# A CIN and MLP kernel: a pair in three groups instead of four, other row pairs copied, and rows taken directly for the first two pairs

## The chip, the core and the metric

The kernel runs on one core of one Trainium2 chip, with its engines TensorE (PE in the profile; PEld is its weight load), VectorE (DVE), ScalarE (ACT), GpSimd (POOL) and SyncE (SP), and the core's 16 DMA engines. The metric is the device time of one execution in microseconds, as the median of a few runs.

## The reference

An xDeepFM network on 512 samples: 26 embedding rows of 32 numbers each, two layers of a compressed interaction network (CIN), a deep network of three layers, and a linear part. Constants: B = 512, M = 26, E = 32, ND = 13, layers of 128 outputs in the CIN, 1024, 512 and 256 in the deep network.

```python
emb = tables[feat_idx, sparse]                     # (B, 26, 32)
linear_out = lin_sparse_w[feat_idx, sparse].sum(-1) + dense @ lin_dense_w
x0 = xk = emb
for w, bb in ((conv1_w, conv1_b), (conv2_w, conv2_b)):
    h = xk.shape[1]
    hp = jnp.einsum('bhd,bmd->bhmd', xk, x0).reshape(-1, h * M, E)
    xn = jax.nn.sigmoid(jnp.einsum('oi,bid->bod', w, hp) + bb[None, :, None])
    half = xn.shape[1] // 2
    xk = xn[:, :half]
    res.append(xn[:, half:])
cin_out = (jnp.concatenate(res, axis=1).sum(-1) @ cin_w + cin_b)[:, 0]
deep_x = jnp.concatenate([emb.reshape(-1, M * E), dense], axis=-1)
h1 = jnp.tanh(deep_x @ W1 + b1)
h2 = jnp.tanh(h1 @ W2 + b2)
h3 = jnp.tanh(h2 @ W3 + b3)
return linear_out + cin_out + (h3 @ deep_w + deep_b)[:, 0] + bias[0]
```

## The kernel before

**Tiling.** The 512 samples are cut into 16 pairs of blocks (`NPAIR`); a block has 16 samples, which are 512 columns (`CH`, 16 samples by 32 dimensions). The two blocks of a pair are called c = 0 and 1. GpSimd gathers the rows of pair i with seven indirect DMAs (`gather`, line 372) into `emb`, where a partition is one field of one sample. SyncE writes them to `laid` in HBM, one row per field (`lay_out`, lines 293 and 295), and reads them back in two forms: as `raw`, 26 rows in four places (`fetch`, line 307), and as `copied`, each of two rows spread over 64 partitions (`copy`, line 318; 512 KB for one tile in two transfers). `x` is made from `raw`: ScalarE's `x_high` (line 611) rounds it to the fast format, VectorE's `x_low` (line 730) puts the rest beside it, so that `x` holds a high and a low part of each row.

**First CIN layer.** By squares: `sums_of(i, u)` (line 439, three for each pair) forms sums of two rows with a selection matrix, `squares` (line 620) squares them, `layer1(i, c)` (line 457, twelve matmul records each) multiplies them by weights, `sigmoid(i, c)` (lines 631 and 633) gives `xk` and `res1`.

**Second CIN layer.** Thirteen tiles for each pair, of two rows of x0 by 64 rows of `xk`. The left factor of a tile is either one of `copied`, from the DMA, or is spread by TensorE with `spread_tile` (line 469) from `x` into a PSUM bank; `COPIED` and `SPREAD` say which. VectorE multiplies it by `xk` (line 800), and `main(r)` (line 479, four matmul records) adds weights times product to the bank `conv`. Then `sigmoid2` (line 641) and the folds over dimensions (`fold1_of`, `fold2_of`, lines 738 and 744).

**Deep network.** The weights of layer 1 are split into high and low parts piece by piece (`piece_high`, `piece_low`), one piece for each pair from pair 1 on. `turn` (lines 757 and 758) transposes `emb` into `xt`; ScalarE makes `xt_hi` (line 695) and GpSimd `xt_lo` (line 381); for the last pair they are made apart (lines 698, 699 and 388). `deep(layer, mt)` (line 500) multiplies in three passes: high by high, low by high, high by low; `deep(0, 0)` has 21 matmuls.

**Order.** Each engine's order is written out by hand. From pair 1 on TensorE goes through `GROUPS` (lines 563 to 575): for each group first the sums of a later pair (`SUMS_IN`) and the spreads (`SPREADS_IN`), then the tiles of the group, then one half of the next pair's layer 1 after groups 0 and 1 (`L1_IN`). Pair 0 has an order of its own (lines 543 to 561). Sums and spreads share three PSUM slots of two banks in turn (`RING`): a slot taken by a spread is free when VectorE has multiplied it, one taken by sums when ScalarE has squared them. Sums and spreads use 58 rows at partition 0 and 58 at partition 64, so c = 0 and c = 1 run in two row halves; `main` and `layer1` use 64 weight columns each, in two column halves. There are six `copied` buffers (`RC`) for seven copied tiles in a pair: `copy(n)` waits for `main` of the tile of copy n - 6, and SyncE issues everything in order, with `lay_out(i + 3)` after the second and `fetch(i + 3)` before the fifth copy of a pair. There are three `prod` buffers (`RP`), one of which is free when `main` of the spread tile three earlier is done. VectorE goes through tiles 0 to 12, with side work behind certain tiles (lines 803 to 814). GpSimd's `gather(i)` waits until the rows of pair i - 1 are in. `WARM` matmuls run at the start on data that is at hand.

## Time and profile before

| | |
|---|---|
| runs | 426.15, 426.61, 427.26 us, median 426.61 |
| profiled execution | 427.28 us, its span 425.20 us |
| PE busy | 406.2 us (96%) |
| DVE busy | 312.3 us (73%) |
| ACT busy | 160.9 us (38%) |
| POOL busy | 166.6 us (39%) |
| moved by DMA | 74.12 MB, mean 174 GB/s |
| products of the second layer, line 479 | 832 matmul records |
| layer 1, line 457 | 384 matmul records |
| spreads (line 469), sums (line 439) | 192 and 96 matmul records |

Times in the trace are microseconds from the start of the span. Consecutive matmuls overlap, so a row's length is more than its share of TensorE's time; from one start to the next is what it takes. A row with `x12` stands for twelve instructions in a run.

### The profile page before, as it was taken

Reading aid. Unit: us, or ns where it says so; the run is one execution under the profiler, and the core shown is the slowest. Engines: PE = TensorE matmul, PEld = TensorE weight load, DVE = VectorE, ACT = ScalarE, POOL = GpSimd, SP = SyncE. Lnnn points to the kernel's source line nnn. Section 1 sums busy time; section 2 is a strip of 40 time slices with the busy share of each in tenths; the row PEclk is TensorE's granted clock in tenths of the full one; section 3 lists DMA queues with packets and bytes.
Section 4 is the critical chain, followed back from the end, with each engine's and each line's share of the span. In section 5 each row is a group of like instructions: output and inputs, shape, how many; then the busy total and the mean of one; then the engine's idle time right before and its main releaser. Section 6 shows DMA issues by size and latency. Waiting matters only on the chain.

```text
span 425.2 us, 5237 instructions
## 1 busy us (share of the span) xinstructions
PE 406.2 (96%) x1850; PEld 164.2 (39%) x1850; DVE 312.3 (73%) x345; ACT 160.9 (38%) x269; POOL 166.6 (39%) x148
## 2 busy tenths in 40 slices
PE   3968999989999999999999999999999989999997
PEld 1322333323333333333333333333333326887885
DVE  4006977979989889898989898988989893732223
ACT  3054343435444435436262534443543601111112
POOL 6752662463643735645748340000000371870000
PEclk9996999999999999999999999999999999999999
DMA  5458679998999999999899999988876940330000
GB/s 200 84 119 184 162 168 226 228 228 216 227 239 236 237 226 231 232 223 237 212 233 221 229 211 229 216 207 205 208 193 163 224 115 0 102 98 2 0 0 1
DMA packets 42176, 74.12 MB, mean 174 GB/s; under 512 B 20593, under 2 KB 23025, under 8 KB 42150
## 3 DMA queue, kind: packets, MB, share of 16 engines
q1 hardware_dynamic: 38566, 72.03, 71.1%
q0 software_dynamic: 3584, 1.76, 3.1%
q8 instruction: 14, 0.23, 0.2%
q14 instruction: 12, 0.10, 0.1%
HBM read 72.06 MB, written 1.71 MB: 173 GB/s over the span
## 4 chain that ended last, share of the span: by engine, by line
PE 77%; DMA 8%; POOL 6%; DVE 4%; issue 3%; SPq 2%; DVEq 0%
PE conv L479 36%; PE conv L457 16%; PE conv L500 8%; PE ring L500 7%; POOL emb L372 6%; PE ring L469 5%; DMA emb<-in_table,rows 4%; PE ring L439 4%; DMA copied<-laid 4%; DVE copied L800 2%; SPq L318 1%; DVE prod L800 1%; PE ring L514 1%; DMA idx_sb<-in_idx 0%; SPq L307 0%
## 5 line engine op out<-in xcount | busy, mean ns | idle before, releaser
L372 POOL DMA_INDIRECT emb<-in_table,rows x112 | 133.9, 1196 | 114.8 <-DMA emb<-in_table,rows 83.1
L800 DVE TENSOR_TENSOR copied<-copied,xk 128x1024 f32<-128x1024 f32 x112 | 134.0, 1226 | 5.4 <-DMA copied<-laid 5.2
L800 DVE TENSOR_TENSOR prod<-ring,xk 128x1024 f32<-128x1024 f32 x96 | 115.4, 1220 | 30.2 <-PE ring L469 28.3
L479 PE MATMUL conv<-copied,w_sb 128*64 128x512 f32 x448 | 105.9, 594 | 3.9 <-DVE copied L800 3.7
L479 PE MATMUL conv<-prod,w_sb 128*64 128x512 f32 x384 | 98.5, 619 | 1.1 <-DVE prod L800 1.1
L631 ACT ACTIVATE xk<-conv,const_sb 64x512 f32<-64x512 f32 x64 | 43.6, 682 | 128.9 <-PE conv L457 128.0
L457 PE MATMUL conv<-sq,w_sb 117*64 117x512 f32 x384 | 88.1, 593 | 0.3 <-ACT sq L660 0.3
L620 ACT ACTIVATE sq<-ring 117x512 f32<-117x512 f32 x90 | 48.6, 594 | 27.3 <-PE ring L439 25.2
L479 PEld LDWEIGHTS conv<-copied,w_sb 128*64 128x64 f32 x448 | 31.2, 137 | 69.5 <-issue 46.2
L457 PEld LDWEIGHTS conv<-sq,w_sb 117*64 117x64 f32 x384 | 27.2, 136 | 54.2 <-issue 54.0
L381 POOL TENSOR_TENSOR xt_lo<-xt,xt_hi 128x480 fp32r<-128x480 f32 (+1 forms) x7 | 9.4, 1366 | 88.7 <-ACT xt_hi L695 84.1
L479 PEld LDWEIGHTS conv<-prod,w_sb 128*64 128x64 f32 x384 | 22.0, 137 | 42.3 <-issue 34.3
L469 PE MATMUL ring<-x,sel_sb 58*128 58x512 f32 x192 | 35.7, 419 | 0.7 <-ACT sq L620 0.7
L730 DVE SCALAR_TENSOR_TENSOR x<-raw,const_sb,x 122x512 fp32r<-122x512 f32 x16 | 12.0, 751 | 23.7 <-ACT x L611 23.7
L439 PE MATMUL ring<-x,sel_sb 58*117 58x512 f32 x96 | 23.6, 494 | 3.7 <-DVE x L730 3.7
L469 PEld LDWEIGHTS ring<-x,sel_sb 58*128 58x128 f32 x192 | 16.8, 186 | 21.2 <-issue 16.2
L439 PEld LDWEIGHTS ring<-x,sel_sb 58*117 58x117 f32 x96 | 8.7, 178 | 42.0 <-issue 38.7
L633 ACT ACTIVATE res<-conv,const_sb 64x512 f32<-64x512 f32 x32 | 21.8, 683 | 0.8
L835 DVE CAST h_hi<-hf 128x512 fp32r<-128x512 f32 x8 | 8.6, 1075 | 18.0 <-ACT hf L711 18.0
L641 ACT ACTIVATE res<-conv,const_sb 128x512 f32<-128x512 f32 x16 | 11.0, 688 | 22.9 <-PE conv L479 22.9
L611 ACT ACTIVATE x<-raw 122x512 fp32r<-122x512 f32 x16 | 10.2, 636 | 21.6 <-DMA raw<-laid 21.5
L744 DVE TENSOR_REDUCE fold<-res 128x16 f32<-128x512 f32 x16 | 10.2, 639 | 6.6 <-ACT res L641 6.6
(98 smaller groups left out, 298.7 us busy)
## 6 DMA issues: line engine op xcount, KB each, us to landing
copied<-laid SPq DMA_DIRECT2D x224, 256.0 KB, 5.5
wpiece<-in_mlp SPq DMA_DIRECT2D x22, 256.0 KB
raw<-laid SPq DMA_DIRECT2D x64, 52.0 KB
emb<-in_table,rows POOLq DMA_INDIRECT x112
laid<-emb SPq DMA_DIRECT2D x16, 96.0 KB
sel_f<-in_sel SPq DMA_DIRECT2D x1, 832.0 KB, 6.1
const_sb<-in_const SPq DMA_DIRECT2D x1, 626.5 KB, 4.5
w_sb<-in_w SPq DMA_DIRECT2D x1, 416.0 KB, 6.6
```

The source lines that it names most:

```text
L372: pool.indirect_dma_start(out=emb[0:n, i, j, :], out_offset=None, in_=table, in_offset=bass.IndirectOffsetOnAxis(ap=rows[0:n, i, j:j + 1], ...
L439: mm = nc.tensor.matmul(sums_bank(i, u)[0:UK, c, :], sel1_sb[at:at + XK, u, :], x[i % RX][at:at + XK, :], start=True, stop=True)
L457: mm = nc.tensor.matmul(l1_bank(i, c)[o, :], w1_sb[:, u, o], sq[i % 2][0:UK, u, c, :], start=(u == 0), stop=(u == UT - 1))
L469: mm = nc.tensor.matmul(spread_bank(r)[:, c, :], sel2_sb[at:at + XK, t, :], x[i % RX][at:at + XK, :], start=True, stop=True)
L479: mm = nc.tensor.matmul(conv[i % 2][c * HALF:(c + 1) * HALF, :], w2_sb[:, t, :], prod_of(r)[:, c, :], start=(t == 0), stop=(t == T2 - 1))
L500: mm = nc.tensor.matmul(MLP_BANKS[n % 2], w[0:r, k, mt * P:(mt + 1) * P], h[0:r, k, :], start=(k == 0 and j == 0), stop=(k == kt - 1 and j ...
L620: nc.scalar.activation(sq[i % 2][0:UK, u, c, :], sums_bank(i, u)[0:UK, c, :], ACT.Square)\
L631: nc.scalar.activation(xk[i % 2][q * HALF:(q + 1) * HALF, c, :], bank[0:HALF, :], ACT.Sigmoid, bias=small_sb[0:HALF, C_CB1:C_CB1 + 1]).the ...
L633: nc.scalar.activation(res1[i % 2][c * HALF:(c + 1) * HALF, :], bank[HALF:P, :], ACT.Sigmoid, bias=small_sb[HALF:P, C_CB1:C_CB1 + 1]).then ...
L641: nc.scalar.activation(res2[i % 2][:, :], conv[i % 2][:, :], ACT.Sigmoid, bias=small_sb[:, C_CB2:C_CB2 + 1]).then_inc(l2_read, 1)
L730: nc.vector.scalar_tensor_tensor(x[i % RX][0:XEND, :], raw[i % RX][0:XEND, :], small_sb[0:XEND, C_LOW:C_LOW + 1], x[i % RX][0:XEND, :].bit ...
L800: nc.vector.tensor_tensor(prod_of(r)[:, :, :].rearrange("p c n -> p (c n)"), left[:, :, :].rearrange("p c n -> p (c n)"), xk[i % 2][:, :, ...
```

## The change

The tiles are grouped 4, 5 and 4 instead of 4, 4, 4 and 1, and each group is preceded by one sum and two spreads. Which tiles are copied changes with it: 2, 3, 6, 7, 8, 11, 12 (seven as before). ScalarE's squares and sigmoids of the next pairs stand in the new order. In the last pair `deep(0, 0)` is cut into three parts by `DEEP_IN`, one behind each group, each waiting for the `xt_lo` it reads; the last pair is turned in pair 14, `xt_hi` and `xt_lo` are made whole (seven each), and the folds of pair 14 (second) and 15 come behind the products. For pairs 0 and 1 the rows go from `emb` straight into a staging tile `wide` (the buffers copied4 and copied5, until `x_lo` of the pair is made) by seven transfers that each wait for their own gather, instead of through `laid` and `raw`; `x_high` and `x_low` are then two instructions each, one for each block. Pair 0's and 1's `lay_out` stays, for the copies. Two matmuls on weights, whose result is not used, stand before the first sums of pair 1.

```diff
@@ -36,18 +36,19 @@
...
+DIRECT = 2
...
-COPIED = (2, 3, 5, 6, 7, 10, 11)
+COPIED = (2, 3, 6, 7, 8, 11, 12)
...
-DEEP_AT = 2
-GROUPS = ((0, 1, 2, 3), (4, 5, 6, 7), (8, 9, 10, 11), (12,))
-SPREADS_IN = (((0, 4),), ((0, 8), (0, 9)), ((0, 12), (1, 0)), ((1, 1),))
-SUMS_IN = {0: ((1, 2),), 2: ((2, 0),), 3: ((2, 1),)}
+DEEP_IN = {0: (0, 1), 1: (2, 3), 2: (4, 5, 6)}
+GROUPS = ((0, 1, 2, 3), (4, 5, 6, 7, 8), (9, 10, 11, 12))
+SPREADS_IN = (((0, 4), (0, 5)), ((0, 9), (0, 10)), ((1, 0), (1, 1)))
+SUMS_IN = {0: ((1, 2),), 1: ((2, 0),), 2: ((2, 1),)}
...
@@ -206,6 +208,20 @@
...
+        def wait_rows(eng, i):
+
+            if i < DIRECT:
+                for j in range(GJ):
+                    eng.wait_ge(early_in[i][j], 16)
+            else:
+                eng.wait_ge(rows_in[i % GSEM], ROWS * (i // GSEM + (1 if i % GSEM >= DIRECT else 0)))
+
+        wide = [copied[RC - DIRECT + k] for k in range(DIRECT)]
+
+        def raw_landed(i):
+
+            return RAW * (i // RX + (1 if i % RX >= DIRECT else 0))
...
@@ -289,11 +305,19 @@
 
             def lay_out(i):
 
-                sp.wait_ge(rows_in[i % GSEM], ROWS * (i // GSEM + 1))
+                wait_rows(sp, i)
...
+            def direct(i):
+
+                for j in range(GJ):
+                    m = GM if j < NG else ML
+                    sp.wait_ge(early_in[i][j], 16)
+                    sp.dma_start(wide[i][j * GM:j * GM + m, :, :].rearrange("p c n -> p (c n)"),
+                                 emb[0:m * PB, i, j, 0:E]).then_inc(wide_in[i], 16)
...
@@ -314,6 +338,8 @@
                 if n >= RC:
                     sp.wait_ge(main_done, tile_of_copy(n - RC) + 1)
                 sp.wait_ge(laid_in[i % RX], LAID * (i // RX + 1))
+                if RC - DIRECT <= n < RC:
+                    sp.wait_ge(x_lo_done, n - (RC - DIRECT) + 1)
...
@@ -324,12 +350,12 @@
...
+            direct(0)
             lay_out(0)
-            fetch(0)
             for n in range(2):
                 copy(n)
+            direct(1)
             lay_out(1)
-            fetch(1)
...
@@ -363,30 +389,21 @@
...
-                if i >= GSEM:
-                    pool.wait_ge(rows_in[i % GSEM], ROWS * (i // GSEM))
                 if i >= 2:
-                    pool.wait_ge(rows_in[(i - 1) % GSEM], ROWS * ((i - 1) // GSEM + 1))
+                    wait_rows(pool, i - 1)
...
+                    ).then_inc(early_in[i][j] if i < DIRECT else rows_in[i % GSEM], 16)
...
@@ -401,16 +418,15 @@
...
-            pool.wait_ge(prod_done, T2 * (NPAIR - 2) + 12)
-            for k in range(3):
+            pool.wait_ge(prod_done, T2 * (NPAIR - 1))
+            for k in range(2):
                 xt_low(k)
             pool.wait_ge(prod_done, T2 * (NPAIR - 1) + 4)
-            for k in range(3, 5):
+            for k in range(2, 4):
                 xt_low(k)
-            pool.wait_ge(prod_done, T2 * (NPAIR - 1) + 8)
-            for k in range(5, K1):
+            pool.wait_ge(prod_done, T2 * (NPAIR - 1) + 9)
+            for k in range(4, K1):
                 xt_low(k)
-            xt_low_rest()
...
@@ -483,16 +499,16 @@
...
-            def deep(layer, mt):
+            def deep(layer, mt, ks=None):
 
                 hi, lo, kt, xh, xl = deep_layers[layer]
                 start = sum(MT[:layer])
                 n = start + mt
-                if n == 0:
-                    pe.wait_ge(xt_lo_done, K1 + 2)
                 if n >= 2:
                     pe.wait_ge(tanh_done, n - 1)
-                for k in range(kt):
+                for k in range(kt) if ks is None else ks:
+                    if n == 0:
+                        pe.wait_ge(xt_lo_done, k + 1)
...
@@ -500,7 +516,8 @@
...
-                mm.then_inc(mlp_done, 1)
+                if ks is None or ks[-1] == kt - 1:
+                    mm.then_inc(mlp_done, 1)
...
@@ -540,6 +557,10 @@
...
+            slot_free("sums", 1, 0)
+            for k in range(2):
+                nc.tensor.matmul(sums_bank(1, 0)[:, 0, :], w2_sb[:, 0:2, :].rearrange("p t o -> p (t o)"),
+                                 w2_sb[:, 0:8, :].rearrange("p t o -> p (t o)"), start=True, stop=True)
             for u in range(UT):
                 sums_of(1, u)
                 main(u)
...
@@ -567,10 +588,11 @@
...
-                    if i == NPAIR - 1 and g == DEEP_AT:
-                        pe.wait_ge(piece_lo, KW)
-                        pe.wait_ge(l2_read, NPAIR - 1)
-                        deep(0, 0)
+                    if i == NPAIR - 1 and g in DEEP_IN:
+                        if g == 0:
+                            pe.wait_ge(piece_lo, KW)
+                            pe.wait_ge(l2_read, NPAIR - 1)
+                        deep(0, 0, DEEP_IN[g])
...
@@ -603,7 +625,14 @@
...
-                act.wait_ge(raw_in[i % RX], RAW * (i // RX + 1))
+                if i < DIRECT:
+                    act.wait_ge(wide_in[i], 16 * GJ)
+                    act.wait_ge(zeroed, 2 + i)
+                    for c in range(2):
+                        nc.scalar.activation(x[i][HALF * c:HALF * c + M, :], wide[i][0:M, c, :], ACT.Copy, scale=-1.0)\
+                          .then_inc(x_hi_done, 1)
+                    return
+                act.wait_ge(raw_in[i % RX], raw_landed(i))
...
@@ -682,21 +711,20 @@
...
                 if i + 1 < NPAIR:
                     sigmoid(i + 1, 0)
+                if i + 2 < NPAIR:
+                    squares(i + 2, 0)
+                if i + 1 < NPAIR:
                     sigmoid(i + 1, 1)
                 if i + 2 < NPAIR:
-                    squares(i + 2, 0)
                     squares(i + 2, 1)
...
-                    act.wait_ge(turned, 2 * (NPAIR - 1))
+                    act.wait_ge(turned, 2 * NPAIR)
...
                     for k in range(K1):
                         n = P if k < K1 - 1 else K1_LAST
-                        nc.scalar.activation(xt_hi[0:n, k, 0:XT], xt[0:n, k, 0:XT], ACT.Copy).then_inc(xt_hi_done, 1)
-
-            act.wait_ge(turned, 2 * NPAIR)
-            nc.scalar.activation(xt_hi[:, 0:NG, XT:B], xt[:, 0:NG, XT:B], ACT.Copy).then_inc(xt_hi_done, 1)
-            nc.scalar.activation(xt_hi[0:K1_LAST, NG, XT:B], xt[0:K1_LAST, NG, XT:B], ACT.Copy).then_inc(xt_hi_done, 1)
+                        nc.scalar.activation(xt_hi[0:n, k, :], xt[0:n, k, :], ACT.Copy).then_inc(xt_hi_done, 1)
...
@@ -726,7 +754,15 @@
...
-                dve.wait_ge(x_hi_done, i + 1)
+                if i < DIRECT:
+                    for c in range(2):
+                        at = HALF * c
+                        dve.wait_ge(x_hi_done, 2 * i + c + 1)
+                        low = nc.vector.tensor_tensor(x[i][at + XLO:at + XK, :], wide[i][0:M, c, :],
+                                                      x[i][at:at + M, :].bitcast(F32), ALU.add)
+                    low.then_inc(x_lo_done, 1)
+                    return
+                dve.wait_ge(x_hi_done, DIRECT + i + 1)
...
@@ -804,16 +840,20 @@
...
-                    if t == FOLD1_AT[k]:
+                    if t == FOLD1_AT[k] and i < NPAIR - 1:
                         fold1_of(i)
-                    if t == (0 if i == NPAIR - 1 else TURN_AT):
+                    if t == TURN_AT and i < NPAIR - 1:
                         turn(i)
-                    if t == TURN_AT and i:
+                        if i == NPAIR - 2:
+                            turn(NPAIR - 1)
+                    if t == TURN_AT and 0 < i < NPAIR - 1:
                         fold2_of(i - 1)
...
             nc.vector.tensor_reduce(lin[:, :], emb[:, :, 0:NG, E], AX.X, ALU.add).then_inc(lin_step, 1)
+            fold2_of(NPAIR - 2)
+            fold1_of(NPAIR - 1)
             fold2_of(NPAIR - 1)
             dve.wait_ge(fold1_done, NPAIR)
```

## Rows read from the trace of the kernel before

**Rows 1.** The page: granted clock in 40 slices, and the queue of the gathers.

```profile
PEclk9996999999999999999999999999999999999999
...
q0 software_dynamic: 3584, 1.76, 3.1%
```

**Rows 2.** Busy time of each engine in two stretches, clock, DMA share, GB/s.

```profile
119.64:139.41 19.77, 19.77 (x97) 6.44 (x98) 17.76 (x19) 9.04 (x16) 8.97 (x8) 1.00 1.02 234
...
258.05:277.83 19.78, 19.78 (x97) 6.44 (x98) 17.76 (x19) 8.97 (x16) 0.00 (x0) 1.00 0.92 218
```

**Rows 3.** The chain that ended last, one pair: start us, us, what.

```profile
218.51 1.01 PE conv L479 x4
220.18 3.58 PE conv L479 x16
223.76 2.58 PE conv L457 x12
226.33 0.67 PE ring L469 x3
...
233.16 0.42 PE ring L439 x2
...
234.04 3.58 PE conv L479 x16
238.28 1.01 PE conv L479 x4
```

**Rows 4.** Timeline of one pair: start, us, what [idle before].

```profile
198.78 1.23 DVE L800 TENSOR_TENSOR prod<-ring,xk 128x1024 f32<-128x1024 f32 x1 [1.90 <-PE ring L469]
...
199.92 2.35 DVE L800 TENSOR_TENSOR copied<-copied,xk 128x1024 f32<-128x1024 f32 x2
...
213.44 1.39 ACT L631 ACTIVATE xk<-conv,const_sb 64x512 f32<-64x512 f32 x2 [4.73 <-PE conv L457]
```

**Rows 5.** Line 318 (`copied`) from 100 to 120 us: issue to landing.

```profile
DMA to landing us min/median/max: 3.5/6.4/9.2
```

**Rows 6.** Timeline of the start, from `laid` of pair 1 to tile 0.

```profile
25.59 0.40 SPq L293 DMA_DIRECT2D laid<-emb  x1
...
27.82 1.54 SPq L307 DMA_DIRECT2D raw<-laid  x4
...
31.13 0.63 ACT L611 ACTIVATE x<-raw 122x512 fp32r<-122x512 f32 x1 [3.35 <-DMA raw<-laid]
...
33.21 2.36 DVE L800 TENSOR_TENSOR prod<-ring,xk 128x1024 f32<-128x1024 f32 x2 [0.66 <-ACT xk L631]
...
34.58 1.97 PE L479 MATMUL conv<-prod,w_sb 128*64 128x512 f32 x4 [1.10 <-DVE prod L800]
```

**Rows 7.** Timeline in pairs 1 and 2, and the chain before pair 3.

```profile
54.06 0.39 SPq L293 DMA_DIRECT2D laid<-emb  x1
...
58.80 0.49 PE L439 MATMUL ring<-x,sel_sb 58*117 58x512 f32 x2
...
68.45 1.23 DVE L800 TENSOR_TENSOR copied<-copied,xk 128x1024 f32<-128x1024 f32 x1 [1.14 <-DMA copied<-laid]
...
89.81 1.23 DVE L800 TENSOR_TENSOR copied<-copied,xk 128x1024 f32<-128x1024 f32 x1 [1.32 <-DMA copied<-laid]
...
99.87 1.01 PE conv L479 x4
```

**Rows 8.** Timeline and chain in pair 15, and the page's `xt_lo`.

```profile
337.63 0.51 PE L469 MATMUL ring<-x,sel_sb 58*128 58x512 f32 x2
...
337.88 2.88 DVE L800 TENSOR_TENSOR copied<-copied,xk 128x1024 f32<-128x1024 f32 x2
...
352.89 5.02 PE conv L500 x21
...
359.19 0.50 PE L500 MATMUL ring<-xt_hi,m_hi 128*128 128x512 f32 x1
...
L381 POOL TENSOR_TENSOR xt_lo<-xt,xt_hi 128x480 fp32r<-128x480 f32 (+1 forms) x7 | 9.4, 1366 | 88.7 <-ACT xt_hi L695 84.1
```

More of the change, by code:

```diff
@@ L161, in build @@
         rows_in = [sem(f"rows_in{k}") for k in range(GSEM)]
+        wide_in = [sem(f"wide_in{k}") for k in range(DIRECT)]
+        early_in = [[sem(f"early_in{i}_{j}") for j in range(GJ)] for i in range(DIRECT)]
         laid_in = [sem(f"laid_in{k}") for k in range(RX)]
@@ L189, in build @@
         HT = sum(MT)
-        XT = PB * (NPAIR - 1)
         BH = B // 2
@@ L374, in gather @@
                         in_offset=bass.IndirectOffsetOnAxis(ap=rows[0:n, i, j:j + 1], axis=0),
-                    ).then_inc(rows_in[i % GSEM], 16)
+                    ).then_inc(early_in[i][j] if i < DIRECT else rows_in[i % GSEM], 16)
             def xt_low(k):
@@ L380, in xt_low @@
                 pool.wait_ge(xt_hi_done, k + 1)
-                nc.gpsimd.tensor_tensor(xt_lo[0:n, k, 0:XT], xt[0:n, k, 0:XT], xt_hi[0:n, k, 0:XT].bitcast(F32),
+                nc.gpsimd.tensor_tensor(xt_lo[0:n, k, :], xt[0:n, k, :], xt_hi[0:n, k, :].bitcast(F32),
                                         ALU.subtract).then_inc(xt_lo_done, 1)
-            def xt_low_rest():
-                for j, (n, ks) in enumerate(((P, slice(0, NG)), (K1_LAST, slice(NG, K1)))):
-                    pool.wait_ge(xt_hi_done, K1 + j + 1)
-                    nc.gpsimd.tensor_tensor(xt_lo[0:n, ks, XT:B], xt[0:n, ks, XT:B], xt_hi[0:n, ks, XT:B].bitcast(F32),
-                                            ALU.subtract).then_inc(xt_lo_done, 1)
             def split_piece(k):
@@ L753, in turn @@
             def turn(i):
-                dve.wait_ge(rows_in[i % GSEM], ROWS * (i // GSEM + 1))
+                wait_rows(dve, i)
                 at = i * PB
```

## The prediction

> **What bounds the kernel now.** I read the busy time by stretches first, one stretch per pair of batch blocks. From pair 3 on a pair takes 19.77 us, and TensorE is busy in all of it at full clock, VectorE in 17.76, ScalarE in 9 [rows 2]. The DMA engines stand at a share of about 1.0 while rows are gathered, and at 0.92 once the gathers are over [rows 2]; yet the period is the same in both. So TensorE sets the period, and the DMA engines are close behind it.
>
> Next the chain of waits over one pair shows what TensorE's time is made of [rows 3]. Products (L479) and layer 1 (L457) use two column halves; row-sums (L439) and spreads (L469) use two row halves. Twelve matmuls of layer 1 take 2.58 us, 0.215 each. Sixteen of products should then take 3.44 and take 3.58; four should take 0.86 and take 1.01: entering a column stretch costs 0.145. The row stretches last 0.66 (from 219.52 to 220.18: one sum, one spread), 0.67 (two spreads), 0.88 (a sum, two spreads) and 0.66 (237.62 to 238.28). That fits 0.215 for each sum or spread and 0.235 for entering. One change to rows and back costs 0.38 us, and a pair has four.
>
> Last I read the start and the end. The start waits for data: VectorE's first product begins at 33.21, behind rows that go gather, `laid` in HBM, `raw`, `x` [rows 6], and even in pairs 1 and 2 it waits for copies [rows 7]. In pair 15 no layer 1 is left and VectorE is the limit: its products with their side work end at 352.89, and only then come `deep(0, 0)` and the last product [rows 8].
>
> **Steady pairs.** The work per pair is the same: 13 products and 6 blocks of layer 1 (76 matmuls), 3 sums, 6 spreads. With three stretches: 76 x 0.215 + 3 x 0.145 + 9 x 0.215 + 3 x 0.235 = 19.41 us, against 19.77. Taken from the four stretches themselves, the saving is 0.38; I use 0.37. It holds only if nothing else comes late, so I lay out the new pair, with T = 0 at its first row stretch:
> - Rows 0 to 0.88, products 0-3 and layer 1 to 7.04, rows to 7.92, products 4-8 and layer 1 to 14.94, rows to 15.82, products 9-12 to 19.4.
> - ScalarE needs 1.39 after the second layer 1 for the next pair's `xk` [rows 4], so VectorE's product 0 of the next pair begins at 14.94 + 0.1 + 1.4 = 16.45, which is -2.95 in that pair. Products start 1.13 apart (two in 2.35) [rows 4]. Products 1 to 3 begin at -1.8, -0.7, 0.4; 4 and 5 at 1.6 and 2.7; then `x_low` and `fold1`; 6 to 8 at 5.2, 6.3, 7.5; 9 at 8.6; turn and `fold2`; 10 to 12 to 14.8. The idle 19.41 - 17.76 = 1.65 lies before the next product 0, where 1.90 lies now [rows 4].
> - TensorE wants product 3 at 3.6 (there at 1.6), 8 at 11.5 (there at 8.7), product 4's and 5's banks at 7.04 (free at 3.9), `x_low` of pair i+2 at 7.04 instead of in the third group (there at 4.6). All have 2.4 us or more. Squares follow ScalarE's new order, which is that of the stretches. I charge nothing.
> - Copies: a buffer is free when the tile six copies earlier is multiplied. Tile 8's copy is released at 18.6 (tile 11 done) and its second half issued at 19.8; VectorE wants it at 19.4 + 7.5 = 26.9, 7.1 later, and TensorE suffers only when it lands after 29.6, 9.8 later. Tile 3's has 8 and 10.7. Landings take 6.4 in the middle and 9.2 at worst where transfers are dense [rows 5]. So lateness reaches VectorE and is taken up there.
>
> The saving counts for pairs 3 to 14: 12 x 0.37 = 4.4 us. DMA demand: 0.92 x 19.78 = 18.2 us of engine time per pair without gathers, plus the gathers' 3.1% of 425 over 16 pairs, 0.8 [rows 1, 2]: 19.0 of 19.4. It fits narrowly. For pairs 3 to 8, which still carry the backlog of the start, I take 0.5 off.
>
> **The start.** `direct` takes `x` of pairs 0 and 1 straight from `emb`. Pair 0 gains little, since the warm-up matmuls, the aux product and the sums follow each other on TensorE to 21.5: at most 0.5. Pair 1: the last rows are in at 25.6; now 1.8 us pass from issuing `laid` to issuing `raw`, and `raw` is in by 31.1 [rows 6]. The direct transfers of six blocks have been issued as they came, and only the last small one remains. No row shows such a transfer; the `laid` store reads the same 128-byte pieces and needs 1.8, which I take, between 1 and 4. Then 25.6 + 0.4 + 1.8 = 27.8. Two activations of 512 columns at 0.63 (now one) to 29.1, the sigmoids 1.4: the first product begins at 30.6, 2.6 earlier. The two matmuls put before `sums_of(1, 0)` lie in the idle time before 30 and keep TensorE busy: the first two products of pair 0 now take 1.97 us for four matmuls instead of about 1.0, at a granted clock of 0.6 in that slice [rows 1, 6]. That returns up to 1.8, and pair 0 takes its steps sooner: pair 1 could start near 54 instead of 58.80.
>
> The Trainium skill speaks against the direct rows: DMA: Bandwidth & Descriptors, Specifications, asks for 512 B or more for full rate; its section Why small descriptors are slow limits this to HBM. By the first the 128-byte pieces could take twice the 1.8, first product 1.8 later; by the second nothing changes. The `laid` store, with such pieces, is done in 1.8, so I stay with the row.
>
> But there it meets the next wait. SP issues copies in order, behind `lay_out(3)`, which waits for gather 3 (now 54.06); tile 7's copy of pair 1 lands 14.4 later, at 68.45, and tile 7's of pair 2 at 89.81 [rows 7]. POOL's gathers are a chain of their own, seven issues and a landing. They come earlier only because `raw` for two pairs is gone and copies 2 to 5 are out about 2.4 us sooner, so the landings meet less traffic: I take 2.2, between 0 and 3. The same queue place now belongs to tile 8: it lands at 87.6, product done at 88.9. From tile 8's matmuls to the end of the pair: 0.86 + 2.58 + 0.88 + 3.58 = 7.9, so pair 3 starts at 96.8 instead of 100.9 (99.87 + 1.01) [rows 7]. Gain 4.1; with the bounds of the gathers 1.9 to 4.9; if the copies don't bind at all, 8.2 (pair 1 at 53.8, then two pairs of 19.4).
>
> **The last pair.** `turn(15)` and both folds leave VectorE's stretch, `deep(0, 0)` is split in three. TensorE: rows 0.67, products 0-3 3.6, six matmuls of `deep` (21 take 5.02, so 0.23 each plus about 0.25) 1.6, rows 0.67, five products 4.4, `deep` 1.6, four products 3.6, nine of `deep` 2.3, the lin pair 0.35: 18.8 us. VectorE begins at -2.7 and needs 13 x 1.13 and, beside POOL's `xt_low`, some 0.5 for each couple of copied products (2.88 against 2.35) [rows 4, 8]: it ends at 13.1, 2.2 before TensorE wants product 12. ScalarE's seven `xt_hi` and `sigmoid2(14)` end near 2.4, before the first part of `deep` at 4.3. So 18.8 against 359.19 - 337.63 = 21.56: 2.7 gained. The folds behind the products lie beside `deep(0, 1)`. From 359.19 on nothing changes.
>
> The Trainium skill, SBUF — State Buffer, Who interferes with whom, has a VectorE instruction with two SBUF inputs and a GpSimd one that reads SBUF block each other entirely. Taken literally the pair would lose what rival 5 works out; the rows show 0.5 for two products, so I go by them.
>
> **Sum.** 4.1 + 4.4 - 0.5 + 2.7 = 10.7 us. The profiled execution took 427.28 (span 425.20), so 416.6 for it; the median of the runs is 426.61, 0.67 lower: 415.9.
>
> **Rivals.**
> 1. The DMA engines bind until pair 8. For it: a share of 1.0, and landings to 9.2 [rows 2, 5]. Against it: the period does not notice it now. Then the start gives 1.9, pairs 3 to 8 nothing: 1.9 + 2.2 + 2.7 = 6.8, 419.8. Chance 0.22.
> 2. The start is freed entirely: 8.2 + 4.4 + 2.7 = 15.3, 411.3. For it: tile 8's product is wanted later than tile 7's was. Against it: SP's wait for gather 3. Chance 0.12.
> 3. Slower: tile 8's copy lands too late in every pair, as its margin is 9.8 us where tile 7's release left over 11. Each us of landing beyond 9.8 costs a us in each of 14 pairs; the gain is gone from 10.6, and at 11 it is 16.8 - 10.7 = 6.1 more: 432.7. Against it: only the worst landing now is 9.2. Chance 0.04.
> 4. The change doesn't do what it says in the pairs: a stretch of three costs more than 0.88 or a bank isn't free, and 0.37 per pair isn't there: 420.3. The 0.88 stands in the trace, so 0.05.
> 5. VectorE and POOL exclude each other in pair 15: four copied products (2, 3, 11, 12) wait for an `xt_low` of 1.37 each [rows 8], 5.5 in place of the 1.0 in my schedule. VectorE ends at 17.6, TensorE wants product 12 at 15.3, so 2.3 less gained: 418.2. The rows show 0.5 for two, so 0.05. This is what the rule of the Trainium skill above would make of it.
>
> **How the numbers follow.** The forecast (413.5 to 418) has 0.52. Ends of the start's bounds (1.9 to 8.2) and the rivals 1, 2, 4, 5 give 411.3 to 420.3; I take 411.0 to 420.4. A measurement of this kernel tells 0.3%, 1.3 us, from no change. Faster by that holds in all cases but the third and a mild form of it: 0.94; within 0.02; slower 0.04.
>
> **What would show it.** Stretches of 19.4 us with TensorE busy throughout and three row stretches of 0.88; VectorE idle 1.6 once per pair, ended by ScalarE; first product near 30.6; full clock from 25 to 40; pair 3 near 97; 18.8 from the first row stretch of pair 15 to `deep(0, 1)`. VectorE waiting long for `copied<-laid` in pairs past 3 would prove me wrong.

## The result and the profile after

| | before | changed |
|---|---|---|
| median of the runs | 426.88 us (426.15 to 427.26) | 421.26 us (420.43 to 422.01) |
| profiled execution | 427.28, span 425.20 | 420.59, span 418.8 |
| ratio | | 0.9864, interval 0.9835 to 0.9893 |

The ratio is the changed kernel's time over that of the kernel before, with a 95% interval; so are all ratios below, each against runs of the kernel before on the same chip.

The change gains 5.6 us, half of the 10.7 that was forecast, and 421.26 lies above the range. Later comparisons of the same two kernels on three chips gave ratios of 0.9811, 0.9815 and 0.979. So two things are to be explained: why those are some 2 us short of the forecast, and why this one is 3 us behind them.

**The pairs.** Busy time of two stretches of one pair each in the changed kernel (columns as in [rows 2]), then its timeline across one pair.

```profile
119.85:139.26 19.41, 19.41 (x96) 6.61 (x94) 17.71 (x20) 8.97 (x15) 10.92 (x10) 1.00 1.01 227
276.00:295.41 19.41, 19.41 (x97) 6.62 (x95) 17.61 (x20) 8.97 (x15) 0.00 (x0) 1.00 0.91 216
```

```profile
276.00 0.49 PE L455 MATMUL ring<-x,sel_sb 58*117 58x512 f32 x2
276.33 0.63 PE L485 MATMUL ring<-x,sel_sb 58*128 58x512 f32 x4
...
283.05 0.49 PE L455 MATMUL ring<-x,sel_sb 58*117 58x512 f32 x2
...
290.95 0.49 PE L455 MATMUL ring<-x,sel_sb 58*117 58x512 f32 x2
...
291.06 1.39 ACT L660 ACTIVATE xk<-conv,const_sb 64x512 f32<-64x512 f32 x2 [4.68 <-PE conv L473]
...
292.49 2.36 DVE L836 TENSOR_TENSOR prod<-ring,xk 128x1024 f32<-128x1024 f32 x2 [1.80 <-ACT xk L660]
...
295.41 0.49 PE L455 MATMUL ring<-x,sel_sb 58*117 58x512 f32 x2
```

A pair takes 19.41 us where [rows 2] had 19.77, with TensorE busy in all of it. There are three row stretches; from 276.00 to the next row stretch are 7.05 us (7.04 in the schedule), the next is at 290.95 (14.95, against 14.94), and the first product of the next pair starts at 292.49, 2.92 before its pair (2.95). VectorE's whole idle time is that one gap, 1.80 us, ended by ScalarE. The page's two groups of products say the same for the whole run (columns as in the page's part on groups: count, busy and mean, idle before them and its cause):

```profile
L836 DVE TENSOR_TENSOR prod<-ring,xk 128x1024 f32<-128x1024 f32 x96 | 114.2, 1216 | 32.3 <-ACT xk L660 27.4
L836 DVE TENSOR_TENSOR copied<-copied,xk 128x1024 f32<-128x1024 f32 x112 | 135.1, 1243 | 0.0
```

No copied product waited for its transfer in this execution.

**The start.** Timeline of the changed kernel, from the first sums to the first product, GpSimd's gathers (L396) with it, and ScalarE's `sigmoid2` of pairs 0 and 1, which marks the end of a pair.

```profile
21.47 0.91 POOL L396 DMA_INDIRECT emb<-in_table,rows  x1 [0.30 <-issue]
21.53 0.96 PE L455 MATMUL ring<-x,sel_sb 58*117 58x512 f32 x6
25.16 3.04 ACT L689 ACTIVATE sq<-ring 117x512 f32<-117x512 f32 x6 [6.85 <-remote]
25.90 5.39 PE L473 MATMUL conv<-sq,w_sb 117*64 117x512 f32 x12 [3.42 <-ACT sq L689]
27.07 0.96 POOL L396 DMA_INDIRECT emb<-in_table,rows  x1 [4.70 <-DMA emb<-in_table,rows]
...
32.32 2.79 PE L473 MATMUL conv<-sq,w_sb 117*64 117x512 f32 x12
...
34.58 1.06 POOL L396 DMA_INDIRECT emb<-in_table,rows  x1 [0.30 <-issue]
...
37.39 1.39 ACT L660 ACTIVATE xk<-conv,const_sb 64x512 f32<-64x512 f32 x2 [2.60 <-remote]
38.81 2.36 DVE L836 TENSOR_TENSOR prod<-ring,xk 128x1024 f32<-128x1024 f32 x2 [3.26 <-ACT xk L660]
...
62.47 0.69 ACT L670 ACTIVATE res<-conv,const_sb 128x512 f32<-128x512 f32 x1 [0.63 <-issue]
...
81.91 0.69 ACT L670 ACTIVATE res<-conv,const_sb 128x512 f32<-128x512 f32 x1 [1.25 <-issue]
```

Timeline of the kernel before, its first sums and squares and the first sums of pair 3; then those of the changed kernel's pair 3.

```profile
21.52 0.96 PE L439 MATMUL ring<-x,sel_sb 58*117 58x512 f32 x6
...
22.05 3.04 ACT L660 ACTIVATE sq<-ring 117x512 f32<-117x512 f32 x6 [1.57 <-PE ring L439]
...
100.81 0.49 PE L439 MATMUL ring<-x,sel_sb 58*117 58x512 f32 x2
```

```profile
101.22 0.49 PE L455 MATMUL ring<-x,sel_sb 58*117 58x512 f32 x2
```

The rows are direct, yet the first product starts at 38.81 and not at 33.21 [rows 6]. The sums are done at 22.49, and ScalarE, with nothing else to do, squares them at 25.16. The second half of layer 1 ends at 35.11 and its sigmoid starts at 37.39. In the kernel before the squares began 0.53 us behind the start of the sums (22.05 against 21.52), here 3.6 behind. So twice a finished TensorE result reaches ScalarE over 2 us late, and the profile names no engine of the core as the releaser (`remote`); and as TensorE idles meanwhile, its granted clock stands at half, 1.2 GHz, from 25.4 to 32.2, where twelve matmuls take 5.39 instead of 2.79. Pair 1 begins at 62.4 where it began at 58.80 in [rows 7], and since it and pair 2 then take only 19.4 us each, pair 3 begins at 101.22 against 100.81 (the first sums of the pair in each trace).

**The last pair.** Timeline of the changed kernel, and the page's `xt_lo`.

```profile
332.58 3.53 POOL L405 TENSOR_TENSOR xt_lo<-xt,xt_hi 128x512 fp32r<-128x512 f32 x2 [91.58 <-ACT xt_hi L726]
333.37 3.82 DVE L836 TENSOR_TENSOR copied<-copied,xk 128x1024 f32<-128x1024 f32 x2
333.80 0.72 PE L485 MATMUL ring<-x,sel_sb 58*128 58x512 f32 x4
...
337.11 2.34 DVE L836 TENSOR_TENSOR prod<-ring,xk 128x1024 f32<-128x1024 f32 x2
337.27 2.56 POOL L405 TENSOR_TENSOR xt_lo<-xt,xt_hi 128x512 fp32r<-128x512 f32 x2 [1.16 <-DVE copied L836]
...
345.37 3.77 DVE L836 TENSOR_TENSOR copied<-copied,xk 128x1024 f32<-128x1024 f32 x2
...
352.84 0.50 PE L516 MATMUL ring<-xt_hi,m_hi 128*128 128x512 f32 x1
```

```profile
L405 POOL TENSOR_TENSOR xt_lo<-xt,xt_hi 128x512 fp32r<-128x512 f32 (+1 forms) x7 | 10.9, 1582 | 96.2 <-ACT xt_hi L726 91.6
```

From the first row stretch to `deep(0, 1)` are 352.84 - 333.80 = 19.04 us, against 21.56 in [rows 8]. The span's difference closes: from the start of pair 3 to the first row stretch of pair 15 are 333.80 - 101.22 = 232.58 against 337.63 - 100.81 = 236.82, so twelve pairs give 4.24; with 2.52 here, 0.05 behind `deep(0, 1)` and a start that is 0.41 later that makes 6.4 = 425.2 - 418.8.

Two `xt_lo` take 2.56 beside products whose operand `ring` is a PSUM bank (337.27), and 3.53 where the second meets the first couple of copied products (332.58).

### The profile page after: what moved, and what is told of

It reads as the page before. It is cut to its first block, busy times and chain, and to the rows that moved or that the text cites. A ratio compares the mean times of both kernels' runs of the same rounds, so it can differ in the third digit from the quotient of the medians.

```text
span 418.8 us, 5255 instructions
## 1 busy us (share of the span) xinstructions
PE 402.7 (96%) x1854; PEld 167.9 (40%) x1854; DVE 311.9 (74%) x347; ACT 161.9 (39%) x269; POOL 174.6 (42%) x146
## 4 chain that ended last, share of the span: by engine, by line
PE 88%; issue 4%; ACT 2%; another core or an unknown queue 2%; DMA 1%; SPq 1%; DVE 1%; DVEq 0%; ACTq 0%
PE conv L495 43%; PE conv L473 19%; PE conv L516 8%; PE ring L516 7%; PE ring L485 5%; PE ring L455 4%; ACT xk L660 1%; SPq L319 1%; PE ring L531 1%; ACT x L632 1%; DMA idx_sb<-in_idx 0%; ACT res L662 0%; DMA copied<-emb 0%; DVE prod L836 0%
## 5 line engine op out<-in xcount | busy, mean ns | idle before, releaser
L396 POOL DMA_INDIRECT emb<-in_table,rows x112 | 141.9, 1267 | 96.9 <-DMA emb<-in_table,rows 65.2
L836 DVE TENSOR_TENSOR prod<-ring,xk 128x1024 f32<-128x1024 f32 x96 | 114.2, 1216 | 32.3 <-ACT xk L660 27.4
L495 PE MATMUL conv<-prod,w_sb 128*64 128x512 f32 x384 | 93.1, 605 | 2.7 <-DVE prod L836 2.7
L473 PE MATMUL conv<-sq,w_sb 117*64 117x512 f32 x384 | 90.7, 608 | 3.4 <-ACT sq L689 3.4
L405 POOL TENSOR_TENSOR xt_lo<-xt,xt_hi 128x512 fp32r<-128x512 f32 (+1 forms) x7 | 10.9, 1582 | 96.2 <-ACT xt_hi L726 91.6
L495 PEld LDWEIGHTS conv<-prod,w_sb 128*64 128x64 f32 x384 | 23.3, 136 | 47.3 <-issue 42.8
L485 PE MATMUL ring<-x,sel_sb 58*128 58x512 f32 x192 | 32.1, 407 | 0.7 <-ACT sq L649 0.7
L761 DVE TENSOR_TENSOR x<-copied,x 26x512 fp32r<-26x512 f32 x4 | 2.8, 688 | 23.5 <-issue 15.1
L875 DVE CAST xt_hi<-hf 128x512 fp32r<-128x512 f32 x4 | 1.7, 427 | 17.9 <-ACT hf L739 17.9
L739 ACT ACTIVATE hf<-ring,const_sb 128x512 f32<-128x512 f32 x6 | 4.1, 689 | 26.0 <-PE ring L516 26.0
```

Source lines behind the costliest of these rows:

```text
L396: pool.indirect_dma_start(out=emb[0:n, i, j, :], out_offset=None, in_=table, in_offset=bass.IndirectOffsetOnAxis(ap=rows[0:n, i, j:j + 1], ...
L405: nc.gpsimd.tensor_tensor(xt_lo[0:n, k, :], xt[0:n, k, :], xt_hi[0:n, k, :].bitcast(F32), ALU.subtract).then_inc(xt_lo_done, 1)
L473: mm = nc.tensor.matmul(l1_bank(i, c)[o, :], w1_sb[:, u, o], sq[i % 2][0:UK, u, c, :], start=(u == 0), stop=(u == UT - 1))
L485: mm = nc.tensor.matmul(spread_bank(r)[:, c, :], sel2_sb[at:at + XK, t, :], x[i % RX][at:at + XK, :], start=True, stop=True)
L495: mm = nc.tensor.matmul(conv[i % 2][c * HALF:(c + 1) * HALF, :], w2_sb[:, t, :], prod_of(r)[:, c, :], start=(t == 0), stop=(t == T2 - 1))
L836: nc.vector.tensor_tensor(prod_of(r)[:, :, :].rearrange("p c n -> p (c n)"), left[:, :, :].rearrange("p c n -> p (c n)"), xk[i % 2][:, :, ...
```

## Experiments

The first theory was the forecast's own, that direct rows free the start and the copies bind a little later. The rivals were that direct rows bring nothing because the gathers don't move, and that the direct rows or the two idle matmuls themselves disturb the start.

### Taking parts of the start away, and the direct rows alone

Without direct rows (`e1_nodirect`, again `f2_nodirect`):

```diff
-DIRECT = 2
+DIRECT = 0
-            direct(0)
             lay_out(0)
+            fetch(0)
-            direct(1)
             lay_out(1)
+            fetch(1)
```

Without the two idle matmuls (`e2_nodummy`, again `h3_nodummy`):

```diff
-            slot_free("sums", 1, 0)
-            for k in range(2):
-                nc.tensor.matmul(sums_bank(1, 0)[:, 0, :], w2_sb[:, 0:2, :].rearrange("p t o -> p (t o)"),
-                                 w2_sb[:, 0:8, :].rearrange("p t o -> p (t o)"), start=True, stop=True)
```

`e3_neither` has both edits; `e4_before_direct` is the kernel before with `direct`, `wide` and their waits added, four groups and no idle matmuls.

> The changed kernel, but the rows of pairs 0 and 1 go through laid and raw as before; groups, last pair and the two idle matmuls stay. Theory A (the direct transfers hold up the signals of TensorE at 22 to 25 us and 35 to 37 us): squares of pair 0 begin near 22.1 instead of 25.2, first product near 33 instead of 38.8, TensorE at full clock for layer 1 of pair 0, and the time falls by 1 to 4 us against 421.3. Theory B (the two idle matmuls hold up the signal of layer 1 before them): squares of pair 0 still at 25, time within 1 us of 421.3. Theory C (the start is bound by the gathers, whatever comes before): time within 1 us although the first product is earlier.

> The changed kernel without the two idle matmuls before the first sums of pair 1. Theory A: still 25.2 for the squares, the signal of the second layer 1 of pair 0 still late, time within 1 us of 421.3. Theory B: the sigmoids of that layer 1 begin near 35.2 instead of 37.4, first product near 36.6, time 1 to 2 us less.

> The changed kernel with neither the direct rows nor the two idle matmuls: what is left is the grouping, the copied tiles and the last pair. Theory A: start as before (first product 33.2, pair 1 near 58.8), pairs 19.41 each, pair 15 2.5 us shorter: 427 - 4.4 - 2.5 - up to 0.7 from pairs 1 and 2 = 419.5 to 420. Theory C: the same.

> The kernel before with the direct rows for pairs 0 and 1 and nothing else. Theory A: the squares of pair 0 begin at 25 and the first product after 35, time 1 to 5 us more than 426.9. My forecast of step 1: 2 to 4 us less. Theory C: within 1 us.

All on one chip, where the kernel before took 427.35 us (425.51 to 432.19); the changed kernel itself was not run there:

| | median | ratio, interval |
|---|---|---|
| e1_nodirect | 419.49 | 0.979 (0.9728 to 0.9852) |
| e2_nodummy | 422.95 | 0.9886 (0.9825 to 0.9947) |
| e3_neither | 419.14 | 0.9778 (0.9718 to 0.9838) |
| e4_before_direct | 431.35 | 1.0087 (1.0057 to 1.0117) |

The direct rows cost time here: 3.8 us between e2 and e3, 4.0 between e4 and the kernel before. The idle matmuls gain nothing (e1, which has them, is 0.35 us slower than e3). The profiles show less of the first difference than the medians, since e3's profiled execution, 421.76, is its slowest: pair 3 starts at 99.5 in e1, 102.5 in e3 and 103.0 in e2. The idle matmuls do hold the clock: granted clock in 40 slices of the page, e1 with them, then e2 without.

```profile
PEclk9989999999999999999999999999999999999999
```

```profile
PEclk9987999999999999999999999999999999999999
```

The row of e3 is the same as that of e2. Without the idle matmuls the clock falls twice (in e2 from 26.2 to 29.6 and from 36.4 to 43.2), with them once. But in all four profiles the late signals stand as in the recorded one: squares of pair 0 at 25.05, 25.68, 24.95 and 25.43, with the sums begun at 22.45, 21.92, 22.10 and 21.58. So neither the direct rows nor the idle matmuls make the signals late, and the experiment could not tell what they are worth on a chip without it.

### The same kernels on other chips

> The kernel before, once more, as a control for its profile. Theory D (the hold-up of TensorE's signals at 22 to 25 us belongs to the chip or the execution, not to an edit): squares of pair 0 begin at 25 here too, though they began at 22.05 in the first profile, and the first product near 37. If the hold-up comes from the edits that all four kernels so far shared (the grouping, the copied tiles, the last pair), squares begin at 22.05 and the first product at 33.2 again.

> The changed kernel, once more, beside the kernel before on the same chip. By D the same hold-up in both, ratio 0.984 to 0.989; first product 38 to 39, pairs 19.41.

> The changed kernel with raw and laid for pairs 0 and 1 again. Theory G: the first product comes 2 to 3 us later than with the direct rows, pair 3 begins within 1 us of the same place, so time within 1.3 us of the changed kernel, on either side. My forecast of step 1 has it 4 us slower. Theory A': the direct rows cost time in themselves, 1 to 4 us, as where they were put into the kernel before.

> The kernel before with the direct rows alone, on this chip. Theory G: within 1.3 us of the kernel before, since its pairs 1 and 2 wait for the gathers too. Theory A': 2 to 4 us more than before, again. Forecast of step 1: 2 to 4 us less.

> The changed kernel beside the three others, as their base on this chip: 417.5 to 422, depending on whether TensorE's signals are held up at 22 us here.

> The kernel before, for its start on this chip. If the hold-up of TensorE's signals near 22 us belongs to a chip, all four kernels of this job show it or none does: squares of pair 0 at 22 to 23.3 in all, or near 25 in all. If the kernel before is never held up while changed kernels are on the same chip, it belongs to the programs.

> The changed kernel, for its start on this chip, as g3. Without the hold-up 417.5 to 418.5; with it 420.5 to 422, and the first product at 38 to 39 instead of 31.

| chip | kernel | median | ratio, interval |
|---|---|---|---|
| second | c1_before | 426.06 | 0.9999 (0.9975 to 1.0024) |
| second | c2_after | 418.32 | 0.9811 (0.9789 to 0.9832) |
| third | f2_nodirect | 418.43 | 0.9818 (0.9801 to 0.9835) |
| third | f3_before_direct | 425.52 | 0.999 (0.9971 to 1.0008) |
| third | f4_after | 417.79 | 0.9815 (0.9794 to 0.9836) |
| fourth | g3_before | 426.95 | 1.0004 (0.9985 to 1.0023) |
| fourth | g4_after | 418.23 | 0.979 (0.9759 to 0.9821) |

Timeline of `c2_after` at the start:

```profile
21.47 0.91 POOL L396 DMA_INDIRECT emb<-in_table,rows  x1 [0.30 <-issue]
21.81 0.96 PE L455 MATMUL ring<-x,sel_sb 58*117 58x512 f32 x6
22.34 3.05 ACT L689 ACTIVATE sq<-ring 117x512 f32<-117x512 f32 x6 [4.02 <-PE ring L455]
...
31.13 2.36 DVE L836 TENSOR_TENSOR prod<-ring,xk 128x1024 f32<-128x1024 f32 x2 [0.69 <-ACT xk L660]
...
54.91 0.39 SPq L309 DMA_DIRECT2D laid<-emb  x1
55.17 0.69 ACT L670 ACTIVATE res<-conv,const_sb 128x512 f32<-128x512 f32 x1 [1.02 <-PE conv L495]
...
60.87 1.23 DVE L836 TENSOR_TENSOR copied<-copied,xk 128x1024 f32<-128x1024 f32 x1 [3.48 <-DMA copied<-laid]
...
62.15 1.08 PE L495 MATMUL conv<-copied,w_sb 128*64 128x512 f32 x4 [2.62 <-DVE copied L836]
...
64.70 0.63 ACT L640 ACTIVATE x<-raw 122x512 fp32r<-122x512 f32 x1 [7.88 <-DMA raw<-laid]
```

I had expected the delay here too, with a ratio of 0.984 to 0.989 and the first product at 38 to 39, and both were wrong: the squares follow the sums at once. The first product starts at 31.13 (forecast 30.6) and pair 1 at 55.2 (near 54). Then it is as the forecast said, but harder: SyncE issues `laid` of pair 3 at 54.91, in `c1_before` at 55.12 and in [rows 7] at 54.06. The gathers have come 0.2 earlier than in `c1_before`, where 2.2 was taken. Pair 1, which is 4.6 us earlier than in `c1_before` (59.8), waits for a copy at 60.87, and for `x` of pair 3, whose row-sums the change has moved a group forward, until 64.70. It takes 24.7 us, and pair 3 starts at 99.35 against 100.22: 0.9 us is left of the start. With 4.2 for the twelve pairs and 2.5 for the last one, as in the profile above, that makes 7.6; the spans differ by 7.7 (424.5 and 416.8). In the fourth chip's pair of profiles pair 3 goes from 101.21 to 99.46, a gain of 1.75, and the spans from 425.5 to 416.9. In `f4_after` pair 3 starts at 97.9, and no profile of the kernel before stands beside it.

On the third chip direct rows alone are worth 0.6 us in the changed kernel (f2 against f4) and 0.5 in the kernel before (f3), both within the intervals. Their profiles differ by more: pair 3 starts at 99.9 in f2 and 97.9 in f4; these are the slowest run of the one and the fastest of the other.

### Letting the gathers run ahead

```diff
-                if i >= 2:
-                    wait_rows(pool, i - 1)
+                if i >= 3:
+                    wait_rows(pool, i - 2)
```

GpSimd's `gather(i)` now waits for the rows of two pairs back. If the chain of gathers was the failed step, this alone should give the rest.

> The changed kernel, but gather i waits for the rows of pair i - 2 instead of i - 1. Theory G (pairs 1 and 2 are bound by the chain of gathers, which the direct rows did not move, and which the new grouping needs sooner, since the sums of pair i + 2 stand in the second group): gather 3's rows are in by 44 to 48 us instead of 55, pair 1 takes under 21 us instead of 24.7, pair 3 begins near 95 instead of 99.4, and the time falls by 3 to 5 us against the changed kernel of this job. Theory E (the DMA engines are full from 60 us on and take the rest): the rows come sooner, but VectorE waits for copies in pairs 2 to 6, and the gain is under 1 us.

> The changed kernel with the gathers one pair further ahead, and without the direct rows. Theory G (the direct rows gain nothing because the gathers end last behind them): once the gathers are ahead the direct rows show their gain, so this one is 2 to 4 us slower than the one with both (413.4). If the direct rows are worth nothing in any case: within 1 us of 413.4.

> The kernel before with the gathers one pair further ahead and nothing else. Theory G: pairs 1 and 2 take 19.8 us instead of 20.6 and 21.4, so 2 to 2.5 us less than the kernel before; less than the 4.4 that the changed kernel gained, since only there the second group asks for the rows early. If the gathers bind both alike: 4 us less.

`f1_gather_ahead` (the changed kernel with the edit, third chip): 413.43 us, ratio 0.9706 (0.9686 to 0.9726), 4.4 below `f4_after` of the same chip. `g1_nodirect_ahead` (fourth chip): 417.54, 0.9788 (0.9756 to 0.9821), 0.7 below `g4_after`. `g2_before_ahead` (the kernel before with the edit, fourth chip): 425.39, 0.9963 (0.9943 to 0.9983), 1.6 below `g3_before`; in the profiles its pair 3 starts 2.2 earlier (99.05 against 101.21), as was expected of it. Busy time by stretches (columns as in [rows 2]), of `c2_after` and of `f1_gather_ahead`:

```profile
60.00:80.00 20.00, 17.85 (x78) 5.86 (x80) 17.02 (x19) 7.50 (x13) 10.10 (x10) 0.91 1.02 239
```

```profile
60.00:80.00 20.00, 20.00 (x98) 6.75 (x96) 18.25 (x21) 9.19 (x16) 16.00 (x14) 1.00 1.04 231
80.00:100.00 20.00, 20.00 (x100) 6.86 (x98) 19.23 (x22) 9.09 (x15) 16.34 (x13) 1.00 1.04 248
```

In `f1` `laid` of pair 3 is issued at 46.2 and TensorE has no gap: pairs 1, 2 and 3 start at 55.1, 74.5 and 93.9, each 19.4 apart, at a DMA share of 1.04. Pair 3 is 4.0 earlier than in `f4_after` (97.9), and that is the whole difference of the two profiles (413.22, 417.16). This shows the failed step, and it refutes rival 1: at that share the pairs keep their 19.4. It also prices the direct rows when the copies aren't late: pair 1 starts at 59.2 in `g1` and at 55.1 in `f1`, on two chips, though.

### Gathers ahead once more, on one chip

To have direct rows and idle matmuls priced side by side, four kernels ran on a fifth chip. `h1_ahead` is `f1` again, `h2_nodirect_ahead` is `g1` again, `h4_ahead_nodummy` is `h1` without the idle matmuls.

> The changed kernel with each gather waiting for the rows of two pairs back instead of one. Theory A (the failed step of the forecast is that the chain of gathers doesn't move, and direct rows pay only when it does): ratio 0.970 again, pair 3 at 93.9, and 3.5 to 4 us faster than h2. Theory B (the 4 us between the two versions seen before came from two different chips): within 1 us of h2.

> As h1, but the first two pairs' rows go through laid and raw instead of directly. Theory A: ratio 0.979, pair 3 near 98, half clock once between 35 and 40. Theory B: ratio within 0.002 of h1.

> The changed kernel without the two idle matmuls ahead of the first row-sums of pair 1. If they keep the clock up at first products, as the forecast said, the clock falls to half for one stretch near 31 to 40, and pair 1 starts near 57 instead of 55.1; but since pair 1 then waits for copies until 79 to 80 anyway, pair 2 starts at the same time and the whole is within 0.5 us of the changed kernel (ratio 0.981). If their worth is real to the end, ratio 0.985.

> h1 without the two idle matmuls. With the copies no longer late, what pair 0 loses stays lost: forecast 1.8 us by the step on the clock, ratio 0.9745 against h1's 0.970, pair 1 at 57. If the idle matmuls do nothing for the clock, ratio as h1.

| | median | ratio, interval |
|---|---|---|
| h1_ahead | 539.09 | 1.2592 (1.2539 to 1.2645) |
| h2_nodirect_ahead | 537.47 | 1.2534 (1.2488 to 1.258) |
| h3_nodummy | 424.56 | 0.9891 (0.985 to 0.9932) |
| h4_ahead_nodummy | 538.86 | 1.2583 (1.2534 to 1.2632) |

The kernel before took 429.13 (426.22 to 430.63) there. No expectation had this: the kernel that was the best on the third chip is 26% slower than the kernel before on the fifth, in all six runs. From h3 to h4 one wait of GpSimd is changed, and it costs 114 us. Timeline of `h1_ahead`:

```profile
50.24 3.85 PE L473 MATMUL conv<-sq,w_sb 117*64 117x512 f32 x12
...
79.55 1.39 ACT L660 ACTIVATE xk<-conv,const_sb 64x512 f32<-64x512 f32 x2 [30.52 <-remote]
...
124.52 1.39 ACT L660 ACTIVATE xk<-conv,const_sb 64x512 f32<-64x512 f32 x2 [41.56 <-remote]
125.94 2.36 DVE L836 TENSOR_TENSOR prod<-ring,xk 128x1024 f32<-128x1024 f32 x2 [42.23 <-ACT xk L660]
...
144.24 0.90 POOL L396 DMA_INDIRECT emb<-in_table,rows  x1 [0.31 <-issue]
```

The last of the two halves of layer 1 of pair 0 is done at 54.1, the first before 50.24; their sigmoids start at 79.55 and 124.52, and ScalarE has nothing else to do but `x` of pair 1, some 2 us. What ScalarE and VectorE finish is taken up at once: the product follows the sigmoid by 1.42 us (125.94), as in `after` (38.81 behind 37.39), and layer 1 follows the squares of 46.54 at 47.19. Late are the signals of TensorE alone. The profile puts such waits down to `remote`, a word that stands in no profile from the second, third and fourth chip. From the page of `h1_ahead`, then of `h3_nodummy`, GpSimd's busy share and the granted clock in 40 slices; then GpSimd's gathers over the first 150 us, of `h1_ahead` and of `h3_nodummy` (count, busy and mean, idle before them and its cause):

```profile
POOL 6777777777600000000000000000000003477000
PEclk9955755556658999999999999999999999999999
```

```profile
POOL 6744656547547436548558000000000155870000
PEclk9978799999999999999999999999999999999999
```

```profile
L396 POOL DMA_INDIRECT emb<-in_table,rows x112 | 107.0, 956 | 35.9 <-issue 33.8 <-DVE rows L805 2.1
```

```profile
L396 POOL DMA_INDIRECT emb<-in_table,rows x76 | 88.5, 1164 | 59.3 <-DMA emb<-in_table,rows 37.2 <-issue 20.1 <-DVE rows L801 2.0
```

With the edit GpSimd issues all 112 gathers one behind the other, 1.25 us apart, until 145, and never waits for rows. Until then TensorE's results are seen by ScalarE and VectorE 13 to 70 us late; from 180.9 on pairs end 19.4 us apart. In `h3`, where the gathers pause for 37.2 us in all, the start is late by some us, a little more than in the recorded run (first product 41.35 against 38.81). The small delays lie near gathers too. In the changed kernel 14 gathers are issued without a break until 22.4, the squares come at 25.16, in the pause; the next seven end at 35.6 and the late sigmoid starts at 37.39. In the four profiles of the first chip the same seven end between 34.7 and 35.9, the sigmoid starts between 35.5 and 37.5. In `c2_after` the gathers stand at the same places, and nothing is late. The placing is only a reading, and it does not fit everywhere: in the recorded profile the sigmoid at 31.39 follows its matmuls by 0.1 while gathers are being issued, and in `h3` the late squares begin at 27.30, 28.99 and 30.40, amid seven gathers (25.62 to 34.0).

## Why the prediction was wrong, point by point

**Bound and steady pairs: right.** 19.41 us, row stretches of 0.88, TensorE busy in all of it, the next first product 2.92 ahead, one gap of VectorE ended by ScalarE. Pairs 19.4 us apart stand in every profile of a kernel with three groups (one pair of `e1` takes 19.8). The twelve pairs gave 4.24 where I had 4.4. The 0.5 taken off for a backlog was not needed: `f1` runs at 19.4 from pair 1 on with a DMA share of 1.04.

**Last pair: right within 0.25 us, with a term mis-sized.** 18.8 forecast, 19.04 measured. VectorE's two copied products beside GpSimd take 3.82 and 3.77, not 2.88, so contention is 1.5 for two where I had 0.5: 2.9 for both couples, between my 1.0 and the 5.5 of rival 5. I took 0.5 from a couple that had an `xt_lo` beside it for only part of its length: in the kernel before three `xt_lo` run from 334.95 to 338.54 and the couple starts at 337.88, an overlap of 0.66. In the new order a whole `xt_lo` falls into each couple. One alone takes 1.28 (half of 2.56), the longest 2.31; a couple and an `xt_lo` that shut each other out entirely would take 2.35 + 1.28 = 3.6, and they took 3.8. That agrees with the rule of the Trainium skill behind rival 5 (SBUF — State Buffer, Who interferes with whom: such instructions block each other entirely). The rival's mechanism was right, and only its count was too high, since one `xt_lo` meets each couple and not each product. Most of it doesn't reach the end, because VectorE still ends its products at 349.1 and TensorE its own at 350.3; 0.2 does, in products 0 to 3, which take 3.80 (334.45 to 338.25) where I had 3.6.

**The direct rows themselves: right.** In `c2` the last of pair 1's seven transfers is issued by 26.9 and `x` begins at 28.41, 1.5 later at most, within the 1.8 taken. The Trainium skill's rule for 512 B (DMA: Bandwidth & Descriptors, Specifications) would have made it 3.6 by my reckoning; as far as one small transfer can tell, the trace agrees with the section that confines it to HBM (Why small descriptors are slow).

**The failed step: "I take 2.2, between 0 and 3" for the gathers.** They came 0.2 and 0.7 earlier: `laid` of pair 3 at 54.91 and 55.01 in the changed kernel on the second and fourth chip, against 55.12 and 55.71 (52.99 against 54.06 in the recorded profiles). I had reasoned that less traffic lets them land sooner, with no row that showed it; GpSimd's chain (seven issues, a landing, a wait, seven more) is itself the clock there. Second, I looked for the late copy in VectorE's products, while `x` of pair 3, moved a group forward, was the last to come (64.70). So the start is worth 0.9 and 1.75 us in the two pairs of profiles, in place of 4.1 and below the bound of 1.9, and the time is 418 in place of 415.9, inside the range. `f1`, with one wait of GpSimd changed, gives the missing 4 us back (413.43 against 417.79).

**What took it out of the range: a wait that no row of before had.** On the chip of the recorded comparison signals out of TensorE came 2 to 3 us late, twice, and the clock fell in between: a delay that my 30.6 put at nothing. (A third such wait of ScalarE, before 129.36, costs nothing: that pair takes 19.4 like the others.) The recorded profile's pair 3 starts 1.9 later than in `c2`, and that is the 2.0 between their spans (418.8 and 416.8); the medians differ by 3. My first product at 30.6 (31.13 in `c2`) and "full clock from 25 to 40" held on the other chips but not here. Late signals alone do not make the loss, though. In `e1` they are as late, the rows go through `laid`, and 0.979 is as good as the 0.9818 of `f2`, which has none; 0.986 to 0.989 stands only where late signals and direct rows meet (the recorded comparison, e2, h3). Part of how they meet can be read: direct rows bring the sums earlier (21.53 against 22.45 in `e1`) but not the squares (25.16, 25.05), so TensorE idles 3.42 instead of 2.38, the first half of layer 1 takes 5.39 instead of 4.06 at the lower clock, and the first product starts at 38.81 instead of 36.96. The two profiles are from two chips, and no run isolates it.

**The idle matmuls.** They hold the clock, as the four profiles show, but gained nothing where tried: with them the kernel was 0.35 us slower (e1 against e3) and 0.2 slower (h1 against h4), within the noise, both on chips with late signals. On a chip without late signals they were not priced alone.

**Rivals.** 1 fell with `f1`. 2 (411.3, everything freed) is nearly what `f1` does with one more edit, 413.4. 3 and 4 didn't occur. 5 was right in mechanism, too high in its count, and nearly harmless in place.

**What stays open.** Why signals are late on some chips and not on others, and whether it is the gathers' issue or the descriptors that they leave behind that stands in the way: in `h1` two signals came 12 and 19 us after the last gather. That the long delays come with unbroken gathers is shown by h3 and h4, on one chip; that unbroken gathers are enough is refuted by f1, which has them too and no late signal. The link of the small delays to gathers is argued from their times alone. Whether the kernel before has late signals on such chips was seen in no profile; its runs there spread to 432.19 and 430.63. Why direct rows cost 4 us on the first chip is known only in the part told above. On the fifth, with everything held up, h1 is 1.6 slower than h2, so the question for which h1 and h2 were made, what direct rows are worth with early gathers on one chip, has no answer.

## What to carry to other kernels

When an edit makes one chain earlier, list every other chain that joins it next, and look for each in the trace at its own pace: a gather chain of issue, landing and wait doesn't move because its neighbours got lighter. A wait that looks like idle time on a side engine may be what leaves room for others: take it away only after runs on several chips, since the version that was best on one (0.97) was the worst on another (1.26). Of the tested kernels the changed one as it is, or without direct rows (0.979 and 0.9818 on two chips), is the one to keep.
